# Which blocks of the attention weights are transposed by DMA and which on TensorE: 60 moves a pair instead of 40, with a new written order

## The reference

```python
x = x + attn(layernorm(x))      # q, k, v from latents, rope on half of each head
#   scores = q k^T * 128**-0.5, causal mask, attn = softmax(scores), out = attn v, then @ Wo
x = x + ffn(layernorm(x))       # W_q = clip(round(W / mean|W|), -1, 1) * mean|W|
#   silu(x Wup^T) * (x Wgate^T), then @ Wdown^T
```

## Time and profile before

| | us |
|---|---|
| median of three runs | 1763.58 |
| the profiled execution | 1764.33 |
| its span, first to last instruction | 1762.5 |
| PE busy | 1697.7 (96%) |
| DVE busy | 1205.6 (68%) |
| ACT busy | 1049.9 (60%) |
| POOL busy | 834.9 (47%) |
| DMA queue q1 (SP's transfers), share of 16 engines | 50.4% |

### The profile page before, as it was taken

The page is one execution under the profiler, slowest core; times in us unless marked ns, Lnnn a source line. Parts: engine busy times, 40 slices in busy tenths (PEclk is TensorE's granted clock), DMA queues, the critical chain, the costliest instruction groups (busy, mean ns, idle before and its releaser), DMA issues.

```text
span 1762.5 us, 30735 instructions
## 1 busy us (share of the span) xinstructions
PE 1697.7 (96%) x9762; PEld 1367.1 (78%) x9762; DVE 1205.6 (68%) x2815; ACT 1049.9 (60%) x2543; POOL 834.9 (47%) x635
## 2 busy tenths in 40 slices
PE   6899997899999999999999999999999999999998
PEld 5788775677777777777877877877887778888887
DVE  6466775588778787788888888888888733334332
ACT  3233334688788787778787787778777522323222
POOL 2466565344345368677677677577565300000000
PEclk9999998899999999999999999999999999999999
DMA  3399987887677665667657657557555630000000
GB/s 128 114 229 220 237 221 203 184 199 146 144 154 143 125 130 131 145 132 148 125 129 148 128 120 157 123 123 151 121 107 126 192 143 1 25 1 25 0 25 24
DMA packets 390010, 225.94 MB, mean 128 GB/s; under 512 B 305888, under 2 KB 339808, under 8 KB 389600
## 3 DMA queue, kind: packets, MB, share of 16 engines
q1 hardware_dynamic: 378336, 203.05, 50.4%
q10 hardware_dynamic: 11520, 20.98, 4.3%
HBM read 97.06 MB, written 54.53 MB: 86 GB/s over the span
## 4 chain that ended last, share of the span: by engine, by line
PE 61%; POOL 9%; ACT 4%; issue 3%; DVE 3%; DMA 2%; SPq 0%; ACTq 0%; POOLq 0%; DVEq 0%
PE ps_scores L1650 15%; PE ps_o L1710 14%; PE ps_scores L1872 13%; PE ps_scores L1728 7%; PE ps_scores L1691 5%; PE ps_scores L1887 3%; PE ps_o L1887 3%; POOL halved L1217 3%; ACT probs L1457 2%; POOL below L1414 2%; POOL signs L1418 1%; POOL k_lo L1359 1%; POOL signs L1422 1%; DMA signs<-in_W_up 1%; ACT halved L1468 1%
## 5 line engine op out<-in xcount | busy, mean ns | idle before, releaser
L1457 ACT ACTIVATE probs<-ps_scores,bias 128x512 f32<-128x512 f32 (+3 forms) x640 | 397.9, 628 | 106.5 <-DVE bias L1561 85.7
L1217 POOL TENSOR_TENSOR halved<-probs,halved 128x512 f16<-128x512 f32 (+3 forms) x320 | 320.9, 1017 | 251.8 <-ACT halved L1468 240.5
L1710 PE MATMUL ps_o<-moved,kv_hi 128*128 128x256 f16 x2176 | 335.0, 275 | 0.6 <-DMA moved<-halved 0.6
L1551 DVE TENSOR_REDUCE negmax<-ps_scores 128x1 f32<-128x512 f32 (+1 forms) x384 | 251.5, 673 | 52.6 <-PE ps_scores L1650 52.4
L1710 PEld LDWEIGHTS ps_o<-moved,kv_hi 128*128 128x128 f16 x2176 | 184.2, 98 | 96.8 <-issue 73.9
L1650 PE MATMUL ps_scores<-k_hi,q_hi 128*128 128x512 f32 (+2 forms) x576 | 244.2, 424 | 7.7 <-ACT probs L1457 7.0
L1473 ACT CAST moved<-ps_scores 128x512 f16<-128x512 f32 (+3 forms) x320 | 167.6, 524 | 102.9 <-PE ps_scores L1691 100.4
L1599 DVE TENSOR_TENSOR moved<-ps_scores,moved 128x512 f16<-128x512 f32 (+3 forms) x320 | 193.4, 604 | 48.2 <-ACT moved L1473 46.9
L1650 PE MATMUL ps_scores<-k_hi,q_lo 128*128 128x512 f32 (+2 forms) x576 | 214.1, 372 | 0.0
L1710 PE MATMUL ps_o<-moved,kv_lo 128*128 128x256 f16 x1088 | 213.2, 273 | 0.0
L1650 PE MATMUL ps_scores<-k_lo,q_hi 128*128 128x512 f32 (+2 forms) x576 | 213.1, 370 | 0.0
(11 more groups left out here) (165 smaller groups left out, 3513.7 us busy)
## 6 DMA issues: line engine op xcount, KB each, us to landing
plainT<-plain_out ACTq DMA_DIRECT2D x64, 256.0 KB, 4.5
rotT<-rot_out SPq DMA_DIRECT2D x64, 256.0 KB, 4.4
all_signs<-signs SPq DMA_DIRECT2D x24, 512.0 KB, 3.2
q_raw<-plainT SPq DMA_DIRECT2D x128, 64.0 KB, 2.4
q_raw<-rotT SPq DMA_DIRECT2D x256, 32.0 KB, 2.1
signs<-in_W_up SPq DMA_DIRECT2D x16, 512.0 KB, 4.2
signs<-in_W_gate SPq DMA_DIRECT2D x16, 512.0 KB, 3.9
signs<-in_W_down SPq DMA_DIRECT2D x16, 512.0 KB, 4.0
```

Source lines behind the costliest of these rows:

```text
L1217: nc.gpsimd.tensor_tensor(halved_of(args, pair, 1), by_block(probs_of((n, i, 0, p), pair)), halved_of(args, pair, 0), ALU.subtract).then_i ...
L1457: nc.scalar.activation(probs_of(args, pair), ps_scores[:, pieces.number[args] % RING, 0:keys], ACT.Exp, scale=-1.0 if last_piece(*args) el ...
L1551: nc.vector.tensor_reduce(to, scores, AX_X, ALU.max, negate=True).then_inc(max_done, 1)
L1710: last = nc.tensor.matmul(ps_o[:, i, 0:2 * P], kv[x][:, b, :], there, start=(s == 0 and (m, b) == (0, blocks[0])), stop=(s + 1 == nsteps(t ...
```

## The change

A new function `by_dma` sends a piece through the DMA when it is of the first head, of the small tile, or the third piece of a large tile. These pieces of the second head leave the turns and become moves. The halved buffers are now counted by piece and head, and the units of `moved` by piece, with a head in each half. A piece's ring buffer `probs` is given back by POOL's `halved_lo` where it is moved, and by PE's turn where it is turned.

```diff
+def by_dma(n, i, h, p):
+    return h == 0 or i == 1 or p == 2
...
-                for p in range(npieces(t)):
-                    for kind in ("halved_hi", "halved_lo", "move", "turn", "turned_hi", "turned_lo"):
-                        put(kind, i, p)
+                        for kind in (("halved_hi", "halved_lo", "move") if by_dma(n, i, h, p) else
+                                     ("turn", "turned_hi", "turned_lo")):
+                            put(kind, i, h, p)
...
-    moved_in = [sem(f"moved_in{j}") for j in range(MOVED)]
+    moved_in = [sem(f"moved_in{j}") for j in range(HALVED)]
...
     def moved_of(args, pair):
-        return moved[(moves.total(args, pair) - 1) % MOVED][:, 0:nblocks(*args)]
+        n, i, h, p = args
+        return moved[unit_of(n, i, p, pair) % MOVED][:, 0:nblocks(*args), :, h * P:(h + 1) * P]
...
     def until_probs_free(engine, args, pair):
-        n, i, h, p = args
-        if h == 0:
-            engine.wait_ge(halved_lo_ready, lows.total((n, i, p), pair))
+        if by_dma(*args):
+            engine.wait_ge(halved_lo_ready, lows.total(args, pair))
         else:
-            engine.wait_ge(turn_ready, turns.total((n, i, p), pair))
+            engine.wait_ge(turn_ready, turns.total(args, pair))
```

```diff
-                if kind == "abs":
+                if kind == "abs" and args[0] % 2 == 0:      # ACT
...
+                if kind == "abs" and args[0] % 2:           # DVE
+                    n, = args
+                    dve.wait_ge(abs_loaded, 16 * (n + 1))
+                    nc.vector.tensor_reduce(abs_sums[:, n // PAIRS, n % PAIRS:n % PAIRS + 1], signs[:], AX_X, ALU.add,
+                                            apply_absolute_value=True).then_inc(abs_done, 1)
...
-    BEHIND = (2, 3, 4, LAST)
+    BEHIND = (2, 3, USUAL, LAST)
...
-        self.only[0] += [(0.2, 0, "split_w", (0,)), (1.9, 0, "stores_over", ()), (3.5, 0, "load_w_first", (1,)),
-                         (5.0, 0, "split_w", (1,))]
+        self.only[0] += [(0.2, 0, "split_w", (0,)), (0.5, 0, "stores_over", ()), (1.5, 0, "load_w_first", (1,)),
+                         (5.6, 0, "split_w", (1,))]
```

`TIMES` is new as a whole; two of its rows for slot 0 read:

```diff
-            "move": (-6.06, -5.16, -4.26, -3.37, -0.42),
-            "turn": (-3.27, -1.92, -0.52, 1.87, 3.95),
+            "move": (-5.27, -4.28, -3.29, -2.3, -1, -0.01, 0.51),
+            "turn": (-3.19, -1.35, 1.2),
```

More of the change, by code:

```diff
@@ new lines @@
+        {
+            "scores": (-10.37, -9.98, -9.58, -9.18, -7.2, -6.4, -5.6, -5.2, -3.16, -1.61),
+            "maximum": (-9.55, -9.2, -8.84, -8.48, -6.69, -5.66, -5.1, -4.74, -2.31, -1.17),
+            "exp": (-7.98, -7.21, -6.22, -5.84, -4.24, -3.86, -3.49, -2.43, -1.58, -0.69),
+            "halved_hi": (-7.56, -6.56, -5.61, -5.27, -2.78, -1.08, -0.34),
+            "halved_lo": (-7.17, -6.17, -5.23, -4.53, -2.39, -0.75, -0.01),
+            "move": (-6.39, -5.4, -4.41, -3.42, -1.61, -0.12, 0.63),
+            "turn": (-3.81, -2.26, 1.67),
+            "turned_hi": (-3.11, -1.91, 2.28),
+            "turned_lo": (-2.68, -1.53, 2.68),
+            "values": (0.08, 0.88, 2.2, 3, 4.39, 4.79, 6.24, 6.63, 7.28),
+            "o_hi": (6.74, 8.29),
+            "o_lo": (7.19, 10.2),
+            "out": (9.47, 11.13, 12.73, 14.42),
+            "add": (10.41, 11.63, 13.44, 14.92),
+        },
@@ new lines @@
+        {
+            "scores": (-10.31, -9.92, -9.52, -9.12, -7.72, -6.4, -5.61, -5.21, -3.16, -1.52),
+            "maximum": (-9.74, -9.38, -9.02, -8.66, -7.22, -5.9, -5.1, -4.75, -2.32, -0.64),
+            "exp": (-8.24, -7.1, -6.16, -5.78, -4.33, -3.95, -3.57, -2.52, -1.76, -0.08),
+            "halved_hi": (-7.81, -6.5, -5.63, -5.29, -2.86, -1.05, 0.34),
+            "halved_lo": (-7.42, -6.11, -5.24, -4.54, -2.47, -0.66, 0.73),
+            "move": (-6.65, -5.34, -4.35, -3.36, -1.7, 0.11, 1.5),
+            "turn": (-3.81, -1.97, 1.27),
+            "turned_hi": (-3.19, -1.38, 2.69),
+            "turned_lo": (-2.68, -1, 3.01),
+            "values": (0.08, 0.87, 1.33, 2.93, 4.42, 4.82, 6.07, 6.57, 8.21),
+            "o_hi": (7.15, 8.95),
+            "o_lo": (8.42, 9.19),
+            "out": (9.38, 10.97, 12.47, 13.86),
+            "add": (10.01, 11.48, 13.1, 14.43),
+        },
@@ new lines @@
+        {
+            "scores": (-10.44, -10.05, -9.05, -7.65, -6.86, -6.06, -5.86, -4.66, -3.52, -2.72),
+            "maximum": (-9.84, -9.49, -8.75, -7.15, -6.35, -5.76, -5.3, -4.26, -2.87, -2.3),
+            "exp": (-8.25, -7.87, -6.8, -5.26, -4.88, -4.5, -3.67, -2.75, -1.04, -0.66),
+            "halved_hi": (-7.49, -7.15, -6.53, -4.23, -3.09, -2.4, -0.36, 0.18),
+            "halved_lo": (-7.1, -6.4, -5.7, -3.96, -2.71, -2.01, 0.03, 0.73),
+            "move": (-6.33, -5.34, -4.35, -3.48, -1.93, -0.94, 0.8, 1.8),
+            "turn": (-4.37, -1.72),
+            "turned_hi": (-4, -1.37),
+            "turned_lo": (-3.23, -0.99),
+            "values": (-0.68, 0.32, 0.72, 2.21, 3.61, 5.05, 5.85, 7.63, 8.03),
+            "o_hi": (4.11, 8.39),
+            "o_lo": (4.36, 8.63),
+            "out": (9.03, 10.23, 12.22, 13.61),
+            "add": (9.53, 10.76, 12.72, 14.33),
+        },
@@ new lines @@
+        {
+            "scores": (-11.42, -11.02, -9.28, -7.88, -7.09, -6.39, -6.19, -4.99, -3.55, -2.75),
+            "maximum": (-10.87, -10.51, -8.98, -7.38, -6.6, -6.09, -5.63, -4.43, -2.76, -2.25),
+            "exp": (-8.48, -8.1, -7.17, -5.59, -5.21, -4.69, -3.88, -2.82, -0.99, -0.07),
+            "halved_hi": (-7.8, -7.45, -6.9, -4.42, -3.17, -2.4, -0.41, 0.36),
+            "halved_lo": (-7.41, -6.71, -6.15, -4.15, -2.78, -2.01, -0.02, 0.74),
+            "move": (-6.46, -5.47, -4.73, -3.66, -2, -1.01, 0.75, 1.74),
+            "turn": (-4.2, -1.55),
+            "turned_hi": (-3.5, -1.26),
+            "turned_lo": (-3.12, -0.94),
+            "values": (-0.77, 0.83, 1.62, 2.02, 3.62, 5.01, 5.41, 6.26, 6.66),
+            "o_hi": (4.35, 7.18),
+            "o_lo": (5.71, 7.63),
+            "out": (9.4, 11.24, 13.14, 14.58),
+            "add": (10.02, 12.07, 13.83, 15.08),
@@ L1085, in attention @@
     lows, turns = plan.count("halved_lo"), plan.count("turn")
[L1086 removed]
+    units = plan.count("move", lambda n, i, h, p: h == 0)
+    assert highs.number == lows.number == moves.number
     assert turns.number == plan.count("turned_hi").number == plan.count("turned_lo").number
@@ L1708, in body @@
                             p = piece_of(t, b)
-                            there = moved[(moves.total((n, i, p), pair + f) - 1) % MOVED][:, b - cuts(t)[p], z, :]
+                            there = moved[unit_of(n, i, p, pair + f) % MOVED][:, b - cuts(t)[p], z, :]
                             last = nc.tensor.matmul(ps_o[:, i, 0:2 * P], kv[x][:, b, :], there,
```

235 lines of the change are left out of this document (89 added, 146 removed).

## The result

The changed kernel takes 1827.39 us (median of 4 runs, 1823.63 to 1830.59), the kernel before 1762.57 beside it: a ratio of 1.0365, 95% interval 1.0341 to 1.0389. It is 3.65% slower; forecast were 1735 us and a range of 1699 to 1768. The profiled execution has a span of 1821.8 us, 59.3 more than before.

The account below looks back on a forecast made before the run. SP's issue queue was to replace PE as bound, at 129 us plus 1.2 idle in a middle pair against 134; pair changes of -28.8 us from 1764.3 gave 1735.5, 1735 as median, own range 1722 to 1750, wider range 1699 to 1768.

Parts of the forecast that it names:

- What leaves PE: Transposes on PE: 63 of 136 leave each pair, PE gains 7.7 us and needs about 126.3 of 134.
- The loads of POOL, DVE and the DMA engines: Per pair: POOL 94 to 112 us, DVE 110 less 11.2, DMA engines 87 to 110; POOL and DVE stay under 126.
- The queue as the new bound: SP's issue queue: 102 us a pair plus 27.2 for 20 more moves, 129, above PE's 126.3.
- the idle term: Each queue-bound pair: 1.2 us added, what PE idles in a middle pair of the kernel before.
- over the pair I put that at 6.7: SP's queue: time by which issues are held up, put at 6.7 us a pair within the sum of 102.
- The third rival: Full DMA engines hold up SP's queue: held time doubles to 13.4, middle pairs 138.1 us, about 1789 in all; chance 0.16.
- Its reason against: Against full DMA engines holding up the queue: pair 0 already has a DMA share of 0.73 and takes only 135 us.
- the margin of the moves: A tile's first moves stand some five units of 1.75 us ahead of its values, so a late queue can catch up.
- Rival 2: POOL's halvings come late and return `probs` late: 133 us a middle pair, 1747 us in all; chance 0.13.
- less 2 each: In the sum for a late POOL: the pairs other than 3 to 6 gain 2 us less each, giving 1747.
- The sum by pairs: Pairs 3 to 6 -15.6 us, pairs 2 and 7 -7.7 each, pair 0 +4.6, pair 1 -3.4; together -28.8 with +1 at the start.
- under 10 us of waits for POOL in a pair: Sign that the forecast is right: SP's queue waits almost never for POOL; 20 us or more would refute it.

Follow-up runs that it names:

- the run without sign operations: Changed kernel with sign load at 8 units, queries and keys loaded by one transfer, POOL's three sign operations left out: 1698.49 us, ratio 0.9634.
- the three runs in which the queue has three transfers and no chunk holds POOL up: Changed kernel with sign chunk loaded 8 units ahead, 1782.57 us; without sign operations, 1774.57; loaded 8 ahead with sign operations on DVE, 1778.64.
- the load at 8: Changed kernel with the sign chunk loaded 8 units ahead of its comparison instead of 3.2, three transfers kept: 1782.57 us, ratio 1.0112.
- the load at 5: Changed kernel with the sign chunk loaded 5 units ahead of its comparison instead of 3.2, three transfers kept: 1791.21 us, ratio 1.0155.
- the queue relieved: Changed kernel with queries and keys loaded by one transfer instead of three: 1753.36 us with the sign load at 3.2 units, 1735.89 at 8.
- one transfer: Changed kernel with sign load at 8 units and queries and keys in one tensor, loaded by one transfer instead of three: 1735.89 us, ratio 0.9846.

## Why the prediction was wrong

**What leaves PE: right.** 584 single transposes and 480 moves are left, and PE's need is 126.3 us a pair by the forecast, 126.6 in the run in which nothing else is in its way. So the gain was there to be had.

**The loads of POOL, DVE and the DMA engines: right in size.** POOL has 112.1 us in a pair (112), DVE 101 (99). The DMA engines do 0.74 of 147 us, 109 (110). At 0.89 they kept nothing from PE in the run without sign operations, so the rule of the Trainium skill ("VectorE: DVE Perf Modes", the rules for kernel authors), TensorE for a transpose if PSUM will do, did not decide by the engines' time: the price that counted was one issue of 1.26 us or more per move, in SP's queue. Once the queue and the sign work gave room, the 63 blocks by DMA were worth 7.5 us a pair (134.1 to 126.6), against the rule.

**The queue as the new bound: right in kind, too small in size.** The forecast had 129 us of queue and 1.2 us of gaps in a pair, 130.1. Measured are 136.7, 139.0 and 136.6 in the three runs in which the queue has three transfers and no chunk holds POOL up. With the load at 8, pairs 3 to 6, the issues and short gaps take 133.3 us and the longer gaps 3.3. So the queue's own term was 4.3 short and the idle term 2.1. Of the 4.3, 3.0 are the step "over the pair I put that at 6.7", which was held constant: the held-up time is 9.7 us with 60 moves, against 4.1 in the kernel before, so it grew 2.4 times where the moves grew 1.5 times. The rest of the queue's term lies in the other issues and the gaps between them. The third rival came nearest (138.1), but by a held-up time of 13.4 that is too high, and its cause, full DMA engines, is not shown: at a share of 0.89 they kept nothing from PE. Its reason against, the 135 us of pair 0 at a share of 0.73, was weak already in the kernel before: there 7 of 40 issues of pair 0 take over 1.5 us, 9.8 us above 1.26, and did no harm because the longer gaps were 26 us.

**What was not costed: the load of the sign chunk.** The edit from 5 to 3.2 units was not in the sum at all; I took the times of the sign chunks for a detail. This is the larger miss. It costs 8.2 us a pair against the load at 5 (147.1 against 138.9) and 10.4 against the load at 8; the queue's miss was 6.6. The kernel before bore the same edit for 0.4 us a pair, the changed kernel with the queue relieved for 4.2. The forecast had looked at the margin of the moves, some five units, and not at that of every other load in the queue that it declared full.

**Rival 2, POOL late: underrated, and joined to the queue.** It had 133 us a pair; with the queue relieved and the chunk in time a pair takes 131.9, and of these 5.3 go away with POOL's sign operations. Taken away one after the other in pairs 3 to 6: 10.4 us for chunks that come late behind the queue (147.1 to 136.7), 4.8 for the full queue (131.9), 5.3 for the sign operations between short steps, and 126.6 are left for PE. The shares hang on the order in which they are taken: with the queue full, the sign operations' place costs nothing (136.7 with them on POOL, 136.6 on DVE), and with the queue relieved first the late chunks cost 4.2. Pair 2 goes another way: 146.1 in the change, 144.6 with the load at 8, 141.0 with one transfer, 127.1 without sign operations. The rival's 1747 us also has a slip: it is the sum without the "less 2 each" that its text names; with 2 us less gain in each of the four other pairs it would be 1755.

**The sum by pairs.** Pairs 3 to 6 were forecast at -15.6 us and gave +52.0; pair 2 at -7.7 and gave +7.8; pair 7 at -7.7 and gave -2.2; pairs 0 and 1 at +1.2 and gave +1.4. The sign "under 10 us of waits for POOL in a pair" failed as well: SP's waits for POOL are 35.8 us in pair 4 of the changed kernel, and 33.1 with the load at 8, where the gaps over 0.25 us are 3.7. That view counts a wait that runs beside the issuing before it, so it can't tell a full queue from one with room; the gaps between the issues can. The forecast had noted that for the 44 us before, of which 33.3 are gaps over 0.25 us, and set its sign by that view all the same.

## What to carry to other kernels

When a sum says that a queue becomes the bound by 2%, the sum is not done: go through every other thing that the queue issues and ask whose lead it still has, since in an in-order queue at its limit everything is as late as the queue is. Count issues, not bytes: merging three small loads into one was worth 47 us here, and 6 where the queue had room, none of them in the middle pairs. And an engine at 85% in a ring of short steps can cost time already; here it helped to split its long operations over two such engines.

## What the runs showed of the hardware

- A transposing DMA holds SP's queue for 1.26 us at the median, with 40 moves a pair or with 60, in a full queue or in one with room (1.24 with one transfer). The longer ones grow with the number of moves: 7% take over 1.5 us with 40 moves, 16 to 21% with 60, up to 3.1 us in pair 4 of the changed kernel, and the queue's fill makes no difference to that.
- Transfers of 64 bytes between the moves took the packets of 256 bytes from 24 to 38 ns on the mean (the median stayed at 18) and the moves' landing from 3.3 to 6.0 us at the median.
- The comparison over 128x1024 takes 2.85 us on POOL and 0.95 on DVE, a ratio of three, and the subtraction 2.14 and 1.38, a ratio of 1.6. The Trainium skill ("GPSIMD Engine Reference", Engine selection) has operations of one tensor input at about line rate on GpSimd and those of two at half the speed of VectorE. The runs disagree: here the one-input operation is the one with the larger ratio. For the same work the two rows, POOL in the one-transfer kernel and DVE in the one with the first comparison there, 590 to 1340 us:

```profile
L1424 POOL TENSOR_SCALAR below<-signs,bound 128x1024 bf16<-128x1024 f32 x23 | 65.5, 2847 | 0.2 <-POOL k_last_lo L1369 0.2
```

```profile
L1608 DVE TENSOR_SCALAR below<-signs,bound 128x1024 bf16<-128x1024 f32 x24 | 22.8, 952 | 0.0
```
